# Two-layer graph network on one core: the check for uncovered edges stands behind the first two chunks' weights

## The chip, the cores and the metric

The kernel runs on one core of one Trainium2 chip. The metric is the device time of one execution in microseconds (us). An engine is named as the profile names it: PE is TensorE (PEld its weight loads), DVE VectorE, ACT ScalarE, POOL GpSimd, SP SyncE, the last used here only to start transfers. A "q" behind a name (DVEq, ACTq) is that engine's instruction queue: loads of registers, waits, issuing of transfers.

## The reference

There are 3,125 nodes of 64 numbers and 53,125 edges, sorted by their destination node. Two layers follow each other, each with a batch norm, a residual and a layer norm behind it:

```
layer 0: xj  = x[src]                                       # gather by edge
         B   = 8 spline weights per edge, from edge_attr_3
         agg = segment_sum((B (x) xj) @ W[8*64, 64], dst)   # by destination node
         x1  = layernorm(x + elu(batchnorm(agg / count(dst) + x @ root)))
layer 1: agg = segment_sum(x1[src] + edge_attr_64, dst)
         h   = relu(agg @ W1 + b1) @ W2 + b2
         out = layernorm(x1 + batchnorm(h))
```

## The kernel before

The edges lie in 416 tiles of 128; 8 tiles are a chunk (52 chunks), 2 chunks a pair (26 pairs). Since the edges are sorted, the 128 edges of a tile end in few neighbouring nodes: the kernel takes a window of 12 nodes from the first destination of each tile (`base`), and for pairs of tiles a window of 20 nodes. Whether each real edge lies in its window is checked at run time; if one doesn't, every engine takes a slow path at the end of layer 0 (`with ...If(flag > 0)`). With these inputs it isn't taken.

**The start.** SP loads sources, destinations and edge attributes; DVE casts them, PE transposes them (`turn_rows`, L382) so that an edge lies on a partition, DVE makes from them the columns the loop needs: `rel`, `comb`, `srcp` and `turn`. Then comes the check (L818 to L837): some 12 operations of DVE into `missed`, their row sums into `missed_row`, one matmul of PE that adds these over the partitions (L401), and a cast of the sum into `missed_any` (L837), which sets `flag_ready`. Behind it DVE computes the eight spline weights (`basis`, L841 to L851), clears a few tiles (L896 to L903) and builds the one-hot tiles of chunks 0 and 1: `pair` (L877), `ohp` (L880) and `whot` (L863, L867). PE and ACT wait for `flag_ready` before their loops.

**The loop over chunks.** Five engines work side by side, held together by semaphores:

- POOL gathers the rows `x[src]` of each tile by an indirect DMA (`gather_chunk`, L342), in four slots of one chunk each. The 32 gathers of chunks 0 to 3 are written out; a loop over chunks 4 to 15 (L348) and one over 16 to 51 (L351) follow. POOL waits for the list of indices of each pair (`idx_ready`), for the slot (`z_done`), and from chunk 16 on, before each half chunk, for `zsb_ready`, which ACT's copies L656 count up.
- SP loads the rows of `edge_attr_64` into the same slots (L291).
- PE runs `chunk`: per tile a matmul that counts pairs of nodes for layer 1 (L419, with a carry L425 every second tile) and the main matmul `z` (L470) over gathered rows and `whot`; once in a chunk it takes the previous chunk's `z` through the eight kernels (L432, L438), and at its end it counts edges (L443) and turns a tile of `x` or takes it through `root` (L407, L411).
- ACT copies the counted pairs out (`keep_pairs`, L647) and `z` (`keep_z`, L656). At the end of a pair it copies the list of indices for the pair two ahead (`lay_out`, L617). Behind pair 0 it enters its own loop (L676).
- DVE runs `two_chunks`: the one-hot tiles of the chunk two ahead, and `add_windows` (L892), which adds each tile's 12 columns into `agg` at an offset loaded into a register (L885). DVE waits through `m_ready` for PE's matmuls before it overwrites a `pair` tile.

**Behind the loop** PE folds `agg` (L526), DVE and ACT do the batch norm, ELU and layer norm of layer 0, PE does the 300 matmuls of layer 1's sum (L553, L558) while DVE ORs the counts in `adj` to look for an overflow (L1080), and the two last matrices, batch norm and layer norm of layer 1 end the kernel.

The order on each engine is the order in which the code is written. Temporary tiles of the start lie in the space of `adj` (`place`), which ACT fills with counted pairs from its first L647 on. `u` is layer 1's input; until layer 1 its columns hold `xroot` and `xt` and are unused above them.

Of the kernel before, what the change touches and what calls it, by code (L numbers as in the profile page):

```python
# [16 lines left out]
def gnn_two_layers(nc, x, src, dst, ea3, ea64, wk_d, root_d, gamma0, beta0,  # L17
                   w1_d, b1_d, w2_d, b2_d, gamma1, beta1, out):
    P = 128
# [56 lines left out]
    with ctx:  # L76
        def sb(name, shape, dt=F32):
            return ctx.enter_context(nc.sbuf_tensor(name, shape, dt))

        def sem(name):  # L80
            return ctx.enter_context(nc.semaphore(name))
# [14 lines left out]


        place = adj[:, :, :].rearrange("p t w -> p (t w)").bitcast(F32)
        sizes = [BLK * P * D, BLK * P, BLK * P, D * T * 2, T * 4, T, T, T, T, T, T,
                 BLK * P, BLK * P]  # L100
        ends = [sum(sizes[:n + 1]) for n in range(len(sizes))]
        lead = NT * NA // 4 - ends[-1]
        (ea3_rows, src_rows_f, dst_rows_f, w_lohi, w_pair, real, missed, missed2, srcf, srcj, steps_bad,
         src_rows, dst_rows) = (
            place[:, lead + e - n:lead + e] for n, e in zip(sizes, ends))
        ea3_rows = ea3_rows.rearrange("p (b e d) -> p b e d", b=BLK, e=P)
# [15 lines left out]
        hid = rows[:, :, :, :].rearrange("p s t c -> p (s t c)")[:, 0:N]  # L122
        xroot = u[0:PN, 0:(NT + 1) * C].rearrange("p (t c) -> p t c", c=C)
        xt = u[0:C, (NT + 1) * C:(NT + 1) * C + PN]
        x_now = sb("x_now", [PN, C])
        zero = sb("zero", [P, 1])
        ident = sb("ident", [P, P])
# [55 lines left out]
        base_ready = sem("base_ready")  # L183
# [192 lines left out]
        def _(pe):  # L376
# [20 lines left out]
            for d in range(D):  # L397
                turn_rows(ps[:, (0, 1, 7)[d], :], lambda b: ea3_rows[:, b, :, d], ea3_turned)

            pe.wait_ge(missed_ready, 1)  # L400
            nc.tensor.matmul(ps[0:1, 5, 0:1], missed_row[:, 0:1], ones[:, 0:1],  # L401
                             start=True, stop=True).then_inc(missed_summed, 1)

            pe.wait_ge(flag_ready, 1)

            def turn_x():
                nc.tensor.transpose(xt_ps, x_now[:, :], ident[0:PN, 0:PN]).then_inc(xt_turned, 1)  # L407

# [81 lines left out]

            for s in range(SLOTS):
                chunk(0, s, first=(s == 0))
            with pe.Fori(1, NCH // SLOTS) as i:
                for s in range(SLOTS):
                    chunk(i, s)
# [112 lines left out]
        def _(act):  # L608
# [12 lines left out]
            lay_out(CH, CH, CH)  # L621
            for n in range(1, AHEAD // STEP):
                lay_out(n * IDXS, n * IDXS)
            act.wait_ge(flag_ready, 1)

            def copy_x(i):
                nc.scalar.copy(x_now[:, :], x_nm[:, bass.ds(i, 1), :].rearrange("p t c -> p (t c)")).then_inc(x_copied, 1)
# [52 lines left out]
            def copy_fb_idx(layer):  # L680
                with act.Fori(0, T) as t:
                    act.wait_ge(fb_added[layer], t * NR + 1)
                    nc.scalar.copy(fb_idx[:, 0:1], src_col[:, bass.ds(t, 1)]).then_inc(fb_idx_ready[layer], 1)
                    if layer == 0:
                        with act.Fori(0, NR) as r:
# [74 lines left out]
        def _(dve):  # L760
            steps = [0]

            def then_wait(instruction):
                steps[0] += 1
                instruction.then_inc(dve_step, 1)
                dve.wait_ge(dve_step, steps[0])
# [23 lines left out]
            nc.vector.tensor_copy(base[0:1, 0:T], ps[0:1, 5, 0:T])  # L790
# [11 lines left out]
            nc.vector.scalar_tensor_tensor(out=srcp[:, 0:T], in0=srcj[:, :], scalar=-float(PN), in1=srcf[:, :],  # L802
                                           op0=ALU.mult, op1=ALU.add)

            dve.wait_ge(base_ready, 1)
            dve.wait_ge(dst_col_ready, 1)
            dve.wait_ge(base_spread, 1)
            then_wait(nc.vector.tensor_tensor(rel[:, 0:T], dst_col[:, :], ps[:, 6, 0:T], ALU.subtract))  # L810
            group_rel = missed2.rearrange("p (g n) -> p g n", n=GROUP)
            then_wait(nc.vector.tensor_tensor(
                group_rel, dst_col[:, :].rearrange("p (g n) -> p g n", n=GROUP),
                ps[:, 6, 0:T].rearrange("p (g n) -> p g n", n=GROUP)[:, :, 0:1].to_broadcast([P, G, GROUP]),
                ALU.subtract))
            then_wait(nc.vector.scalar_tensor_tensor(out=comb[:, 0:T], in0=srcj[:, :], scalar=float(GWIN),
                                                     in1=missed2[:, :], op0=ALU.mult, op1=ALU.add))
            then_wait(nc.vector.tensor_scalar(real[:, :], dst_col[:, :], 0.0, None, ALU.is_ge))  # L818
            nc.vector.scalar_tensor_tensor(out=missed[:, :], in0=rel[:, 0:T], scalar=0.0, in1=real[:, :],
                                           op0=ALU.is_lt, op1=ALU.mult)  # L820
            nc.vector.tensor_tensor(missed2[:, :], dst_col[:, :], ps[:, 4, 0:T], ALU.is_gt)
            group_step = steps_bad[0:1, 0:G]
            then_wait(nc.vector.tensor_tensor(group_step, base_f[0:1, GROUP:T + 1:GROUP], base_f[0:1, 0:T:GROUP],
                                              ALU.subtract))
            then_wait(nc.vector.tensor_scalar(turn[0:1, :], group_step, 0.0, float(GWIN - 1), ALU.max, ALU.min))
            then_wait(nc.vector.tensor_scalar(group_step, group_step, float(GWIN - 1), None, ALU.is_gt))
            then_wait(nc.vector.tensor_tensor(missed[0:1, 0:G], missed[0:1, 0:G], group_step, ALU.add))
            then_wait(nc.vector.tensor_tensor(srcf[0:1, :], base_f[0:1, 1:T + 1], base_f[0:1, 0:T], ALU.subtract))
            then_wait(nc.vector.tensor_tensor(missed[:, :], missed[:, :], missed2[:, :], ALU.add))
            nc.vector.tensor_scalar(steps_bad[0:1, :], srcf[0:1, :], 1.0, None, ALU.is_lt)  # L830
            then_wait(nc.vector.tensor_scalar(srcf[0:1, :], srcf[0:1, :], float(WIN - 1), None, ALU.is_gt))
            then_wait(nc.vector.tensor_tensor(missed[0:1, :], missed[0:1, :], steps_bad[0:1, :], ALU.add))
            then_wait(nc.vector.tensor_tensor(missed[0:1, :], missed[0:1, :], srcf[0:1, :], ALU.add))
            then_wait(nc.vector.tensor_tensor(missed[0:1, 0:1], missed[0:1, 0:1], base_f[0:1, 0:1], ALU.add))
            nc.vector.reduce_sum(missed_row[:, :], missed[:, :], axis=AX.X).then_inc(missed_ready, 1)
            dve.wait_ge(missed_summed, 1)
            nc.vector.tensor_copy(missed_any[0:1, 0:1], ps[0:1, 5, 0:1]).then_inc(flag_ready, 1)  # L837

            for d in range(D):
                dve.wait_ge(ea3_turned, d + 1)  # L840
# [60 lines left out]
            nc.vector.memset(ln_sum[:, :], 0.0).then_inc(xroot_ready, 1)  # L901
            nc.vector.memset(t_ps, 0.0).then_inc(t_ready, 2)
            then_wait(nc.vector.tensor_copy(iota_p, iota_f[:, 0:WIN]))  # L903
            for c in range(STEP):
                for half in range(2):
                    build_pairs(c, c, half)
                build_weights(c, c)

            def two_chunks(i, first=False):
                for par in range(STEP):  # L910
                    c, after, before = i * STEP + par, i * STEP + (par + STEP), i * STEP + (par - 1)
                    adds = not (first and par == 0)
# [229 lines left out]
```

## Time and profile before

| | |
|---|---|
| median of 3 runs | 677.46 us (676.99 to 678.1) |
| the profiled execution's own time | 677.0 us |
| its span in the profile, first to last instruction | 675.2 us |
| busy: PE, DVE, POOL, ACT | 511.0, 464.3, 399.1, 221.9 us |
| first main matmul on PE | 37.90 us |
| last gather issued by POOL | 529.47 us |
| first matmul of L526, behind the loop | 547.54 us |

No engine is busy for more than 76% of the span. So the shares alone don't say what bounds the kernel; that takes each engine's waits, stretch by stretch. Times in the rows below are from the span's start.

### The profile page before, as it was taken

The page shows a single profiled execution, that of the slowest core. Times are in us where ns is not written, and L with a number is a line of the kernel's source. Part 1 is how long each engine was busy: PE and PEld are TensorE (multiplying, and loading weights), DVE is VectorE, ACT ScalarE, POOL GpSimd, SP SyncE. Part 2 cuts the span into 40 slices and gives each one's busy share as a digit, 9 for nine tenths or more (in the row PEclk, how much of TensorE's full clock was granted, in tenths as well). Part 3 has the DMA queues.
Part 4 walks back from the last instruction along what each step waited for, and adds up shares of the span by engine and source line. Part 5 has one row for each costly group of instructions (what it writes and reads, how often), then busy time and mean ns, then how long its engine had stood idle before and what let it go on. Part 6 is the DMA issues. An engine that isn't in the chain of part 4 may idle for free.

```text
span 675.2 us, 14457 instructions
## 1 busy us (share of the span) xinstructions
PE 511.0 (76%) x3051; PEld 378.7 (56%) x3052; DVE 464.3 (69%) x1606; ACT 221.9 (33%) x478; POOL 399.1 (59%) x423
## 2 busy tenths in 40 slices
PE   5087888788879777888778877888788864699940
PEld 2065766566657556666556656666565663244530
DVE  6996666766766676766666667566666637889376
ACT  4033433433343333333333333333334203410421
POOL 6866777777777777777777777777777400000000
PEclk9996956876697788857885788777868755799975
DMA  5422221212221222122122122122211000000002
GB/s 119 97 61 54 60 58 44 68 45 58 56 58 43 56 56 58 41 58 56 43 56 55 44 58 57 43 56 58 56 41 25 18 2 0 1 1 0 1 1 48
DMA packets 77647, 30.58 MB, mean 45 GB/s; under 512 B 69598, under 2 KB 70971, under 8 KB 77627
## 3 DMA queue, kind: packets, MB, share of 16 engines
q1 hardware_dynamic: 63275, 16.69, 10.7%
q0 software_dynamic: 13312, 13.66, 9.3%
q8 instruction: 8, 0.13, 0.1%
q10 hardware_dynamic: 1040, 0.00, 0.1%
q14 instruction: 12, 0.10, 0.0%
HBM read 29.50 MB, written 0.80 MB: 45 GB/s over the span
## 4 chain that ended last, share of the span: by engine, by line
DVE 27%; PE 27%; issue 17%; POOL 11%; DVEq 11%; DMA 3%; ACT 2%; ACTq 1%; SPq 0%; POOLq 0%
POOL rows L342 11%; PE ps L470 9%; PE ps L419 8%; DVEq L885 7%; DVE agg L892 5%; DVE ohp L880 4%; DVE pair L1080 3%; DMA rows<-in_x,idx 3%; PE ps L438 2%; DVE pair L877 2%; PE ps L526 2%; DVE whot L867 2%; DVE pair L979 1%; DVEq L892 1%; PE ps L558 1%
## 5 line engine op out<-in xcount | busy, mean ns | idle before, releaser
L342 POOL DMA_INDIRECT rows<-in_x,idx x416 | 397.9, 957 | 133.2 <-issue 120.7
L470 PE MATMUL ps<-whot,rows 128*128 128x108 f32 x832 | 224.9, 362 | 74.2 <-DVE whot L867 31.6
L470 PEld LDWEIGHTS ps<-whot,rows 128*128 128x128 f32 x832 | 187.8, 256 | 118.3 <-issue 51.4
L419 PE MATMUL ps<-pair,ohp 128*125 128x500 bf16 x418 | 206.2, 494 | 24.0 <-DVE ohp L880 13.4
L647 ACT CAST adj<-ps 125x500 f32 x208 | 123.7, 595 | 245.6 <-PE ps L425 208.4
L877 DVE TENSOR_SCALAR pair<-iota_h,comb 128x500 bf16<-128x500 int16 x432 | 133.7, 371 | 66.5 <-issue 48.0
L892 DVE TENSOR_TENSOR agg<-agg,ps 128x24 f32 x416 | 74.8, 180 | 93.1 <-issue 41.9
L419 PEld LDWEIGHTS ps<-pair,ohp 128*125 128x125 bf16 x418 | 71.9, 172 | 37.9 <-issue 23.0
L880 DVE TENSOR_SCALAR ohp<-iota_h,srcp 128x125 bf16<-128x125 int16 x432 | 80.9, 277 | 0.0
L867 DVE TENSOR_TENSOR whot<-ps,basis 128x864 f32<-128x864 f32 x54 | 57.1, 1057 | 7.6
L438 PE MATMUL ps<-z_sb,wk 64*64 64x96 f32 x832 | 59.7, 298 | 0.0
L656 ACT COPY z_sb<-ps 128x432 f32<-128x432 f32 x104 | 54.2, 521 | 0.0
L438 PEld LDWEIGHTS ps<-z_sb,wk 64*64 64x64 f32 x832 | 47.6, 168 | 8.8 <-issue 5.7
L425 PE MATMUL ps<-pair,ohp 128*125 x208 | 48.2, 232 | 0.0
L553 PE MATMUL ps<-adj,basis 125*128 125x500 fp8e4 (+1 forms) x175 | 35.0, 362 | 11.0 <-ACT basis L730 11.0
L425 PEld LDWEIGHTS ps<-pair,ohp 128*125 128x125 bf16 x208 | 36.7, 176 | 10.0 <-issue 8.7
L553 PEld LDWEIGHTS ps<-adj,basis 125*128 125x128 bf16 x175 | 16.4, 100 | 29.5 <-ACT basis L730 11.2
L432 PE MATMUL ps<-z_sb,ident 128*64 128x96 f32 x104 | 25.3, 337 | 1.1 <-ACT z_sb L656 1.1
L1080 DVE TENSOR_TENSOR pair<-pair,adj 125x787 int32<-125x787 int32 x23 | 22.5, 978 | 0.8
L640 ACT COPY u<-ps 125x64 f32 (+1 forms) x26 | 5.5, 212 | 48.8 <-PE ps L411 48.8
L631 ACT COPY u<-ps 64x125 f32<-64x125 f32 x26 | 6.7, 258 | 37.2 <-PE ps L407 37.2
L432 PEld LDWEIGHTS ps<-z_sb,ident 128*64 128x64 f32 x104 | 12.9, 176 | 9.1 <-issue 5.5
(148 smaller groups left out, 317.2 us busy)
## 6 DMA issues: line engine op xcount, KB each, us to landing
rows<-in_edge_attr SPq DMA_DIRECT2D x51, 256.0 KB
rows<-in_x,idx POOLq DMA_INDIRECT x416, 2.4
x_nm<-in_x SPq DMA_DIRECT2D x1, 781.2 KB
out<-u SPq DMA_DIRECT2D x3, 218.8 KB
adj<-in_edge_attr SPq DMA_DIRECT2D x1, 576.0 KB
rows<-in_edge_attr SPq DMA_DIRECT2D x1, 224.0 KB
adj<-in_src SPq DMA_DIRECT2D x1, 192.0 KB
adj<-in_dst SPq DMA_DIRECT2D x1, 192.0 KB
```

The costliest lines, as they stand in the source:

```text
L342: pool.indirect_dma_start(rows[:, s, t, 0:C], None, x, bass.IndirectOffsetOnAxis(ap=idx[:, s * CH + t:s * CH + t + 1], axis=0)).then_inc(g ...
L419: return nc.tensor.matmul(m_ps[0:PN, g % MB, 0:PAIRS], ohp[:, par, t, :], pair[:, par, t, :], start=(n == 0), stop=(n == GROUP - 1), skip_ ...
L425: nc.tensor.matmul(m_ps[0:PN, (g + 1) % MB, 0:PAIRS].rearrange("p (j w) -> p j w", w=GWIN)[:, :, 0], ohp[:, par, t, :], bass.AP(pair, offs ...
L438: last = nc.tensor.matmul(t_ps[low:low + C, par, 0:RW], wk[:, k, :], z_of[0:C, :, k, :], start=(k < 2), stop=(k >= NK - 2))
L470: last = nc.tensor.matmul(z_ps[:, half, at:at + ZW], rows[:, s, t, :], whot[:, par, t, :], start=True, stop=True)
L553: nc.tensor.matmul(ps[:, b, 0:min(AB, N - b * AB)], table[:, j, 0:P], adj_part(b, j), start=(j == 0), stop=False, skip_group_check=True)
L647: nc.scalar.copy(bass.AP(adj, offset=start, ap=[[NT * NA, PN], [NA, NT], [1, GWIN]]), m_ps[0:PN, g % MB, 0:PAIRS].rearrange("p (j w) -> p ...
L656: nc.scalar.copy(z_sb[:, par, half * n:(half + 1) * n, :, :], z_ps[:, half, 0:n * ZW].rearrange("p (w k n) -> p w k n", w=n, k=KIN)).then_ ...
L867: nc.vector.tensor_tensor(whot[:, par, :, :].rearrange("p t (k w) -> p t k w", k=KIN), hot[:, :, :].rearrange("p t (a w) -> p t a w", a=1) ...
L877: nc.vector.tensor_scalar(pair[:, par, t, :], iota_h[:, :], comb[:, bass.ds(c * CH + t, 1)], None, ALU.is_equal)
L880: last = nc.vector.tensor_scalar(ohp[:, par, t, :], iota_h[:, 0:PN], srcp[:, bass.ds(c * CH + t, 1)], None, ALU.is_equal)
L892: nc.vector.tensor_tensor(view, view, t_ps[:, par, 0:2 * RW].rearrange("p (a w) -> p a w", a=2)[:, :, t * WIN:(t + 1) * WIN], ALU.add).the ...
```

## The change

The check leaves the start of DVE's stream. What the loop needs (`rel`, `comb`, `turn`) stays. One operation of the check stays as well, since it reads PSUM that is overwritten later: the comparison of the destinations with the next tile's base, now into `beyond`. The rest stands behind `whot` of chunk 1, before DVE's first `two_chunks`, and writes into `check`, three rows of 416 columns in the unused part of `u`. Three pairs of operations on the steps between bases are each joined into one `scalar_tensor_tensor`. PE's matmul over the partitions is issued behind chunk 1, into bank 7; the cast into `missed_any` behind DVE's first `two_chunks`. PE no longer waits for the flag ahead of its loop but behind it; ACT waits ahead of its loop for `base_kept` instead, and for the flag behind it.

```diff
@@ gnn_two_layers
+        check = u[:, (NT + 1) * C + PN:(NT + 1) * C + PN + 3 * T].rearrange("p (n t) -> p n t", n=3)
+        missed, beyond, real = check[:, 0, :], check[:, 1, :], check[:, 2, :]
@@ tensor
-            pe.wait_ge(missed_ready, 1)
-            nc.tensor.matmul(ps[0:1, 5, 0:1], missed_row[:, 0:1], ones[:, 0:1],
-                             start=True, stop=True).then_inc(missed_summed, 1)
-
-            pe.wait_ge(flag_ready, 1)
...
             for s in range(SLOTS):
                 chunk(0, s, first=(s == 0))
+                if s == 1:
+                    pe.wait_ge(missed_ready, 1)
+                    nc.tensor.matmul(ps[0:1, 7, 0:1], missed_row[:, 0:1], ones[:, 0:1],
+                                     start=True, stop=True).then_inc(missed_summed, 1)
...
+            pe.wait_ge(flag_ready, 1)
             flag = pe.value_load(missed_any[0:1, 0:1], min_val=0, max_val=1 << 30)
@@ scalar
-            act.wait_ge(flag_ready, 1)
+            act.wait_ge(base_kept, 1)
...
+            act.wait_ge(flag_ready, 1)
             flag = act.value_load(missed_any[0:1, 0:1], min_val=0, max_val=1 << 30)
@@ vector
-            then_wait(nc.vector.tensor_tensor(rel[:, 0:T], dst_col[:, :], ps[:, 6, 0:T], ALU.subtract))
+            nc.vector.tensor_tensor(rel[:, 0:T], dst_col[:, :], ps[:, 6, 0:T], ALU.subtract).then_inc(rel_ready, 1)
...
-            then_wait(nc.vector.tensor_scalar(real[:, :], dst_col[:, :], 0.0, None, ALU.is_ge))
-            nc.vector.scalar_tensor_tensor(out=missed[:, :], in0=rel[:, 0:T], scalar=0.0, in1=real[:, :],
-                                           op0=ALU.is_lt, op1=ALU.mult)
-            nc.vector.tensor_tensor(missed2[:, :], dst_col[:, :], ps[:, 4, 0:T], ALU.is_gt)
+            nc.vector.tensor_tensor(beyond[:, :], dst_col[:, :], ps[:, 4, 0:T], ALU.is_gt).then_inc(beyond_ready, 1)
...
-            then_wait(nc.vector.tensor_scalar(group_step, group_step, float(GWIN - 1), None, ALU.is_gt))
-            then_wait(nc.vector.tensor_tensor(missed[0:1, 0:G], missed[0:1, 0:G], group_step, ALU.add))
-            then_wait(nc.vector.tensor_tensor(srcf[0:1, :], base_f[0:1, 1:T + 1], base_f[0:1, 0:T], ALU.subtract))
-            then_wait(nc.vector.tensor_tensor(missed[:, :], missed[:, :], missed2[:, :], ALU.add))
-            nc.vector.tensor_scalar(steps_bad[0:1, :], srcf[0:1, :], 1.0, None, ALU.is_lt)
-            then_wait(nc.vector.tensor_scalar(srcf[0:1, :], srcf[0:1, :], float(WIN - 1), None, ALU.is_gt))
-            then_wait(nc.vector.tensor_tensor(missed[0:1, :], missed[0:1, :], steps_bad[0:1, :], ALU.add))
-            then_wait(nc.vector.tensor_tensor(missed[0:1, :], missed[0:1, :], srcf[0:1, :], ALU.add))
-            then_wait(nc.vector.tensor_tensor(missed[0:1, 0:1], missed[0:1, 0:1], base_f[0:1, 0:1], ALU.add))
-            nc.vector.reduce_sum(missed_row[:, :], missed[:, :], axis=AX.X).then_inc(missed_ready, 1)
-            dve.wait_ge(missed_summed, 1)
-            nc.vector.tensor_copy(missed_any[0:1, 0:1], ps[0:1, 5, 0:1]).then_inc(flag_ready, 1)
...
                 build_weights(c, c)
+            dve.wait_ge(rel_ready, 1)
+            dve.wait_ge(beyond_ready, 1)
+            then_wait(nc.vector.tensor_scalar(real[:, :], dst_col[:, :], 0.0, None, ALU.is_ge))
+            then_wait(nc.vector.scalar_tensor_tensor(out=missed[:, :], in0=rel[:, 0:T], scalar=0.0, in1=real[:, :],
+                                                     op0=ALU.is_lt, op1=ALU.mult))
+            then_wait(nc.vector.tensor_tensor(missed[:, :], missed[:, :], beyond[:, :], ALU.add))
+            steps_of_tiles, steps_of_groups = beyond[0:1, :], real[0:1, 0:G]
+            nc.vector.tensor_tensor(steps_of_tiles, base_f[0:1, 1:T + 1], base_f[0:1, 0:T], ALU.subtract)
+            then_wait(nc.vector.tensor_tensor(steps_of_groups, base_f[0:1, GROUP:T + 1:GROUP], base_f[0:1, 0:T:GROUP],
+                                              ALU.subtract))
+            for steps_in, n, bound, op in ((steps_of_tiles, T, 1, ALU.is_lt), (steps_of_tiles, T, WIN - 1, ALU.is_gt),
+                                           (steps_of_groups, G, GWIN - 1, ALU.is_gt)):
+                then_wait(nc.vector.scalar_tensor_tensor(out=missed[0:1, 0:n], in0=steps_in, scalar=float(bound),
+                                                         in1=missed[0:1, 0:n], op0=op, op1=ALU.add))
+            then_wait(nc.vector.tensor_tensor(missed[0:1, 0:1], missed[0:1, 0:1], base_f[0:1, 0:1], ALU.add))
+            nc.vector.reduce_sum(missed_row[:, :], missed[:, :], axis=AX.X).then_inc(missed_ready, 1)
...
             two_chunks(0, first=True)
+            dve.wait_ge(missed_summed, 1)
+            nc.vector.tensor_copy(missed_any[0:1, 0:1], ps[0:1, 7, 0:1]).then_inc(flag_ready, 1)
```

On DVE at the start, this is the stream before, from the group window into `comb` (L812, L816) to the first operation of the spline weights (L841); `adj` stands for every temporary in its space:

```order
L812 TENSOR_TENSOR adj<-dst_col,ps 128x416
L816 SCALAR_TENSOR_TENSOR comb<-adj 128x416
L818 TENSOR_SCALAR adj<-dst_col 128x416
L819 SCALAR_TENSOR_TENSOR adj<-rel,adj 128x416
L821 TENSOR_TENSOR adj<-dst_col,ps 128x416
L823 TENSOR_TENSOR adj<-base_f 1x208
L825 TENSOR_SCALAR turn<-adj 1x208
L826 TENSOR_SCALAR adj<-adj 1x208
L827 TENSOR_TENSOR adj<-adj 1x208
L828 TENSOR_TENSOR adj<-base_f 1x416
L829 TENSOR_TENSOR adj<-adj 128x416
L830 TENSOR_SCALAR adj<-adj 1x416
```

The same place of the stream now, where L824 is the first operation of the spline weights:

```order
L811 TENSOR_TENSOR adj<-dst_col,ps 128x416
L815 SCALAR_TENSOR_TENSOR comb<-adj 128x416
L817 TENSOR_TENSOR u<-dst_col,ps 128x416
L818 TENSOR_TENSOR adj<-base_f 1x208
L820 TENSOR_SCALAR turn<-adj 1x208
L824 TENSOR_SCALAR adj<-ps 128x416 x3
```

L818 and L819 of before are gone from here, and so is all from L826 to L837, six more operations and the cast behind the seven shown: 13 instructions, and the trip over PE.

On DVE behind the weights of chunk 1 (L850, L867 before), ahead of the one-hot tiles of chunk 2 (L860, L877 before), this is what stands there now:

```order
L850 TENSOR_TENSOR whot<-ps,basis 128x864
L897 TENSOR_SCALAR u<-dst_col 128x416
L898 SCALAR_TENSOR_TENSOR u<-rel,u 128x416
L900 TENSOR_TENSOR u<-u 128x416
L902 TENSOR_TENSOR u<-base_f 1x416
L903 TENSOR_TENSOR u<-base_f 1x208
L907 SCALAR_TENSOR_TENSOR u<-u 1x416 x2
L907 SCALAR_TENSOR_TENSOR u<-u 1x208
L909 TENSOR_TENSOR u<-u,base_f 1x1
L910 TENSOR_REDUCE missed_row<-u 128x1
L860 TENSOR_SCALAR pair<-iota_h,comb 128x500 x4
```

Before, L867 was followed at once by L877; now ten operations stand between them.

## Rows read from the trace of the kernel before

**Rows 1.** Part 5 of the page, POOL's gathers (columns as in its head: busy, mean ns).
```profile
L342 POOL DMA_INDIRECT rows<-in_x,idx x416 | 397.9, 957 | 133.2 <-issue 120.7
```
**Rows 2.** Waits: engine line waited for: us in total, times, longest us.
```profile
POOL rows L342 <- ACT idx L617: 5.8, 4, 4.9
...
PE ps L470 <- DMA rows<-in_x,idx: 15.8, 14, 2.4
```
**Rows 3.** Timeline of POOL: start us, us, engine line op, [idle before <-releaser].
```profile
46.77 0.94 POOL L342 DMA_INDIRECT rows<-in_x,idx  x1 [0.31 <-issue]
52.58 0.94 POOL L342 DMA_INDIRECT rows<-in_x,idx  x1 [4.87 <-ACT idx L617]
...
72.59 0.94 POOL L342 DMA_INDIRECT rows<-in_x,idx  x1 [0.30 <-issue]
...
172.73 0.94 POOL L342 DMA_INDIRECT rows<-in_x,idx  x1 [0.30 <-issue]
...
187.82 0.95 POOL L342 DMA_INDIRECT rows<-in_x,idx  x1 [0.30 <-issue]
...
529.47 0.94 POOL L342 DMA_INDIRECT rows<-in_x,idx  x1 [0.31 <-issue]
```
**Rows 4.** Timeline of PE: the last half chunk's wait for gathered rows.
```profile
535.43 0.47 PE L470 MATMUL ps<-whot,rows 128*128 128x108 f32 x2 [2.08 <-DMA rows<-in_x,idx]
```
**Rows 5.** Timeline of DVE at the start.
```profile
14.33 0.38 DVE L818 TENSOR_SCALAR adj<-dst_col 128x416 f32<-128x416 f32 x1
14.74 0.60 DVE L819 SCALAR_TENSOR_TENSOR adj<-rel,adj 128x416 f32<-128x416 f32 x1
15.25 0.58 DVE L821 TENSOR_TENSOR adj<-dst_col,ps 128x416 f32<-128x416 f32 x1
...
16.55 0.26 DVE L826 TENSOR_SCALAR adj<-adj 1x208 f32<-1x208 f32 x1
...
21.53 1.56 DVE L841 TENSOR_SCALAR adj<-ps 128x416 f32<-128x416 f32 x3
```
**Rows 6.** Timeline of PE from the start to the end of chunk 2.
```profile
13.09 3.34 PE L382 MATMUL ps<-ident,adj 128*128 128x128 f32 x12 [0.78 <-DMA adj<-in_edge_attr]
...
37.90 0.73 PE L470 MATMUL ps<-whot,rows 128*128 128x108 f32 x2 [1.58 <-issue]
...
45.12 0.38 PE L419 MATMUL ps<-pair,ohp 128*125 128x500 bf16 x1
...
51.22 0.42 PE L419 MATMUL ps<-pair,ohp 128*125 128x500 bf16 x1
...
56.19 0.65 PE L419 MATMUL ps<-pair,ohp 128*125 128x500 bf16 x1 [3.81 <-ACT adj L647]
...
64.46 0.62 PE L419 MATMUL ps<-pair,ohp 128*125 128x500 bf16 x1
```
**Rows 7.** Windows: us, busy PE, PEld, DVE, ACT, POOL, PEclk, DMA share, GB/s.
```profile
44.46:54.70 10.24, 7.64 (x62) 6.14 (x60) 8.02 (x35) 3.79 (x10) 4.46 (x5) 1.00 0.30 70
54.70:64.94 10.24, 8.75 (x43) 6.97 (x44) 4.89 (x23) 3.34 (x8) 7.65 (x9) 0.50 0.13 27
```
**Rows 8.** Timeline of ACT around the ends of pairs 0, 1 and 2, and chunk 15's copy.
```profile
51.43 0.21 ACT L617 COPY idx<-src_col 128x16 int32<-128x16 int32 x1
55.47 0.57 ACT L647 CAST adj<-ps 125x500 f32 x1 [3.83 <-issue]
...
71.34 0.20 ACT L617 COPY idx<-src_col  x1
...
85.27 0.20 ACT L617 COPY idx<-src_col  x1
...
185.31 0.52 ACT L656 COPY z_sb<-ps 128x432 f32<-128x432 f32 x1
```
**Rows 9.** Timeline of DVE behind the weights of chunk 1, and at its loop.
```profile
42.75 1.32 DVE L877 TENSOR_SCALAR pair<-iota_h,comb 128x500 bf16<-128x500 int16 x4
...
59.63 1.13 DVE L877 TENSOR_SCALAR pair<-iota_h,comb 128x500 bf16<-128x500 int16 x4 [3.23 <-issue]
```

More of the change, by code:

```diff
@@ L98, in gnn_two_layers @@
         place = adj[:, :, :].rearrange("p t w -> p (t w)").bitcast(F32)
-        sizes = [BLK * P * D, BLK * P, BLK * P, D * T * 2, T * 4, T, T, T, T, T, T,
+        sizes = [BLK * P * D, BLK * P, BLK * P, D * T * 2, T * 4, T, T, T, T,
                  BLK * P, BLK * P]
@@ L102, in gnn_two_layers @@
         lead = NT * NA // 4 - ends[-1]
-        (ea3_rows, src_rows_f, dst_rows_f, w_lohi, w_pair, real, missed, missed2, srcf, srcj, steps_bad,
+        (ea3_rows, src_rows_f, dst_rows_f, w_lohi, w_pair, in_group, srcf, srcj, group_steps,
          src_rows, dst_rows) = (
@@ L182, in gnn_two_layers @@
         src_col_ready, dst_col_ready, basis_in = sem("src_col_ready"), sem("dst_col_ready"), sem("basis_in")
-        base_ready = sem("base_ready")
+        base_ready, base_kept, rel_ready, beyond_ready = sem("base_ready"), sem("base_kept"), sem("rel_ready"), sem("beyond_ready")
         base_spread, missed_ready, missed_summed, flag_ready = (
@@ L789, in _ @@
             nc.vector.tensor_copy(base_f[0:1, 0:T], ps[0:1, 5, 0:T]).then_inc(base_ready, 1)
-            nc.vector.tensor_copy(base[0:1, 0:T], ps[0:1, 5, 0:T])
+            nc.vector.tensor_copy(base[0:1, 0:T], ps[0:1, 5, 0:T]).then_inc(base_kept, 1)
             nc.vector.tensor_copy(dst_col[:, :], ps[:, 5, 0:T]).then_inc(dst_col_ready, 1)
@@ L809, in _ @@
             dve.wait_ge(base_spread, 1)
-            then_wait(nc.vector.tensor_tensor(rel[:, 0:T], dst_col[:, :], ps[:, 6, 0:T], ALU.subtract))
-            group_rel = missed2.rearrange("p (g n) -> p g n", n=GROUP)
+            nc.vector.tensor_tensor(rel[:, 0:T], dst_col[:, :], ps[:, 6, 0:T], ALU.subtract).then_inc(rel_ready, 1)
             then_wait(nc.vector.tensor_tensor(
-                group_rel, dst_col[:, :].rearrange("p (g n) -> p g n", n=GROUP),
+                in_group.rearrange("p (g n) -> p g n", n=GROUP), dst_col[:, :].rearrange("p (g n) -> p g n", n=GROUP),
@@ L814, in _ @@
                 ps[:, 6, 0:T].rearrange("p (g n) -> p g n", n=GROUP)[:, :, 0:1].to_broadcast([P, G, GROUP]),
                 ALU.subtract))
-            then_wait(nc.vector.scalar_tensor_tensor(out=comb[:, 0:T], in0=srcj[:, :], scalar=float(GWIN),
-                                                     in1=missed2[:, :], op0=ALU.mult, op1=ALU.add))
-            then_wait(nc.vector.tensor_scalar(real[:, :], dst_col[:, :], 0.0, None, ALU.is_ge))
-            nc.vector.scalar_tensor_tensor(out=missed[:, :], in0=rel[:, 0:T], scalar=0.0, in1=real[:, :],
-                                           op0=ALU.is_lt, op1=ALU.mult)
@@ L821, in _ @@
-            nc.vector.tensor_tensor(missed2[:, :], dst_col[:, :], ps[:, 4, 0:T], ALU.is_gt)
-            group_step = steps_bad[0:1, 0:G]
-            then_wait(nc.vector.tensor_tensor(group_step, base_f[0:1, GROUP:T + 1:GROUP], base_f[0:1, 0:T:GROUP],
-                                              ALU.subtract))
-            then_wait(nc.vector.tensor_scalar(turn[0:1, :], group_step, 0.0, float(GWIN - 1), ALU.max, ALU.min))
-            then_wait(nc.vector.tensor_scalar(group_step, group_step, float(GWIN - 1), None, ALU.is_gt))
@@ L832, in _ @@
-            then_wait(nc.vector.tensor_tensor(missed[0:1, :], missed[0:1, :], steps_bad[0:1, :], ALU.add))
-            then_wait(nc.vector.tensor_tensor(missed[0:1, :], missed[0:1, :], srcf[0:1, :], ALU.add))
-            then_wait(nc.vector.tensor_tensor(missed[0:1, 0:1], missed[0:1, 0:1], base_f[0:1, 0:1], ALU.add))
-            nc.vector.reduce_sum(missed_row[:, :], missed[:, :], axis=AX.X).then_inc(missed_ready, 1)
-            dve.wait_ge(missed_summed, 1)
-            nc.vector.tensor_copy(missed_any[0:1, 0:1], ps[0:1, 5, 0:1]).then_inc(flag_ready, 1)
+            nc.vector.scalar_tensor_tensor(out=comb[:, 0:T], in0=srcj[:, :], scalar=float(GWIN),
+                                           in1=in_group[:, :], op0=ALU.mult, op1=ALU.add)
@@ L839, in _ @@
+            nc.vector.tensor_tensor(beyond[:, :], dst_col[:, :], ps[:, 4, 0:T], ALU.is_gt).then_inc(beyond_ready, 1)
+            then_wait(nc.vector.tensor_tensor(group_steps[0:1, 0:G], base_f[0:1, GROUP:T + 1:GROUP], base_f[0:1, 0:T:GROUP],
+                                              ALU.subtract))
+            then_wait(nc.vector.tensor_scalar(turn[0:1, :], group_steps[0:1, 0:G], 0.0, float(GWIN - 1), ALU.max, ALU.min))
             for d in range(D):
@@ L903, in _ @@
             then_wait(nc.vector.tensor_copy(iota_p, iota_f[:, 0:WIN]))
+            dve.wait_ge(base_kept, 1)
             for c in range(STEP):
```

## The prediction

> **What bounds the kernel now.** I read the costliest groups first. POOL's gathers are one kind of instruction, 416 of them, busy for 397.9 us, with 120.7 us of short gaps between them [rows 1]. So each takes 0.957 + 0.30 = 1.25 us of POOL's stream, 520 us in all: of the 547.5 us until PE begins with L526, the gathers alone need nearly everything. The waits say whether POOL ever stops: for ACT's list of indices it waited 5.8 us in all, and 4.9 of them in one piece [rows 2]. The timeline places that piece: gather 32 starts at 46.77, gather 33 at 52.58, with 4.87 us idle ahead of it [rows 3]. From there to the last gather at 529.47 are 383 steps in 476.89 us, 1.245 us each: no further stop. And PE waits for that stream: 15.8 us in 14 waits for gathered rows [rows 2], the last of them 2.08 us ahead of the last half chunk, until 535.43 [rows 4]. Hence the end of the loop follows POOL, and POOL's stream has one hole. What is won ahead of the loop comes out at the end only as far as gather 33 starts earlier, and as later waits of POOL allow it.
>
> **The start.** In before, 14.33 to 15.25 goes to L818 and L819 (0.92), and 16.55 to 21.53 to everything from L826 to the cast behind the trip over PE (4.98) [rows 5]. Both go: 5.90 us. Edits in what stays (two waits fewer) I set at nothing; they could give up to 0.1. The spline weights then start at 15.63. They read what PE has turned by 13.09 + 3.34 = 16.43 [rows 6]; the three reads lie about 0.5 apart (1.56 for three), the third comes at 16.6 and is not held. Everything up to the one-hot tiles of chunk 0 moves by 5.9, and so does PE's first main matmul, which waits for `whot`: 37.90 becomes 32.0.
>
> **Chunks 0 and 1 on PE.** Chunk 0 takes 45.12 - 37.90 = 7.2 us and would end at 39.2. Chunk 1 took 51.22 - 45.12 = 6.1 [rows 6], nearly all at the higher of the two clock levels: the granted clock is 1.00 (2.4 GHz) in 44.46 to 54.70 and 0.50 (1.2 GHz) in 54.70 to 64.94 [rows 7]. At the lower level six of the eight tiles of chunk 2, with the kernels, took 64.46 - 56.19 = 8.27 [rows 6]; by chunk 0's 0.9 a tile less what stands around it, I estimate a whole chunk at 9.3. Does PE get its higher level at the same instant, though it begins 5.9 us earlier? I assume the same instant, 44.46, as the cautious case. Then 39.2 to 44.46 does 5.26/9.3 = 57% of chunk 1, and the other 43% takes 2.6: end at 47.1, 4.1 earlier than 51.22. Bounds: with the rise earlier too, 45.3 (5.9 earlier); with none, 48.5 (2.7 earlier).
>
> **Gather 33.** The list for pair 2 is ready at 51.43 + 0.21 = 51.64 [rows 8], 4.1 earlier at 47.5 (45.7 to 48.9). POOL itself is through with gather 32 at 47.71 and would start the next at 48.02. Before, 0.94 passed between list and gather [rows 3, 8]; whether that is the wake or part of the loop's entry can't be seen. Between 48.02 and 48.5 I take 48.5: 4.1 earlier than 52.58. Bounds 4.56 (POOL's own pace) and 2.7.
>
> **Gather 49, the next one at risk.** The list for pair 3 was ready at 71.54, 1.05 ahead of gather 49 at 72.59 [rows 3, 8]. Gather 49 would now come at 68.5, so the list must be there by some 68.2, 3.3 earlier. PE's pause until 56.19 waits for ACT, which sat 3.83 us idle on its way into its loop behind L617 [rows 6, 8]; that pause moves with L617, to 52.1. From there to ACT's L617 at 71.34 were 15.15 us, of which 8.75 at the lower level and 6.4 at the higher: 8.75/1.5 + 6.4 = 12.2 us of work at the higher level (9.3/6.1 = 1.5). With the levels at their old instants, 52.1 to 54.70 does 2.6, 54.70 to 64.94 does 6.8, and 2.8 remain: L617 at 67.7, ready at 67.9. Just in time. If the lower level lasted to the end of pair 1 it would be 70.4, and gather 49 would start at about 70.8, 1.8 earlier than before.
>
> **DVE's new piece.** Ten instructions stand between the weights of chunk 1 and the one-hot tiles of chunk 2. From the rows of before [rows 5]: a comparison of 416 columns 0.41 to the next start; six operations of 416 columns with two inputs (the first product, the add, the steps between tiles, two joined ones, the row sums) at 0.60, the longest of those rows, 3.6; two of 208 columns at 0.3 (0.26 and a short gap); one of a single element at 0.2. Together 4.8; with the wait at the head I take 4.9 us. DVE reaches it 5.9 earlier, so the one-hot tiles of chunk 2, at 42.75 before [rows 9], start at 41.8: 1.0 earlier still, so no later than before. PE reaches them 4.1 to 5.9 earlier and could have to wait, but it stands anyway until 52.1 for ACT, and DVE's 1.0 is inside of that. From there on DVE is late in the queue. It began its loop's first tiles at 59.63 behind 3.23 us of idling [rows 9], part of it PE's pause; that idling takes up about 1.4 of the lag. So PE and DVE go into the loop 1 to 3 us ahead of before, POOL 4.1. Who waits for whom there? POOL, from chunk 16 on, waits for ACT's copies of z: the tightest of those waits is before gather 141, at 187.82, whose copy was done at 185.83, 1.99 ahead [rows 3, 8]. With POOL 4.1 earlier it needs the loop 2.1 earlier. I take that as met. Cost of DVE's piece: nothing; without its cover, up to 1 us at gather 141. The matmul behind chunk 1 and the cast behind DVE's first `two_chunks` cost some 0.2 and 0.15, inside the same pauses.
>
> **A rule that speaks against the gain.** Entering the loop at L348 is a taken branch. ACT sat 3.83 us idle on entering its loop, DVE 3.23 [rows 8, 9]; POOL's entry lies in the very 4.87 us that I count as a wait for indices. POOL's second loop begins with gather 129, at 172.73, and there the gap is the usual 0.30 [rows 3]. By the second loop POOL's entry is free, and the sum stands.
> The Trainium skill (Runtime: NRT & Kernel Launch, Instruction fetch mechanics) says that a taken branch to a target outside the pages already held makes the engine fetch the page before it goes on. ACT's idling agrees with it and POOL's second loop doesn't.
>
> **Sum.** 677.0 of the profiled execution less 4.1 = 672.9. Its 677.0 stands 0.46 below the median of before's runs, 677.46; against that median the same gain gives 673.4. Behind the loop nothing is changed: the flag is set hundreds of microseconds ahead. I forecast 673.4; the mechanism's own range is 672.8 (4.6 gained) to 674.5 (3.0).
>
> **Rivals.**
> 1. *Gather 49 or 141 waits.* The lower level of PE's clock, or DVE's lag, holds the loop back and POOL stops a second time. For it: the margins are 1.05 and 1.99 [rows 3, 8]. Against: both need the loop ahead by only 2 to 3 us, out of 5.9. Gain 1.8 to 3.0: about 675.2.
> 2. *The hole is POOL's loop entry.* Then gather 33 comes ACT's 3.3 us (3.83 less its load) behind 47.71, at 51.2, and the gain is 1.4: 676.1, on the edge of no change. For it ACT and DVE, against it the second loop.
> 3. *DVE's piece is the new bound, and the kernel is slower.* If the ten operations, with their waits, took over 7.9 us instead of 4.9, the loop would start more than 2.0 later than before, gather 141 would wait, and each further microsecond would come out at the end. At 10 us, the double, it is 2.1 slower: 679.6. For it: nothing in the rows exceeds 0.60 an operation. Against: ten times the longest row is 6.0.
>
> **How the numbers follow.** Forecast 60%, rival 1 20%, rival 2 11%, rival 3 4%; the other 5% are for what the later clock levels do behind the loop, either way. What a measurement can tell here is 0.2%, 1.35 us. Faster by more: the forecast and rival 1 whole, half of rival 2, half of the rest: 0.87. Within: half of rival 2, a little of rival 3: 0.08. Slower: 0.05. The range leaves out rival 3, the far half of rival 2, and gains over 5.7: 671.8 to 676.0.
>
> **What would show it.** Spline weights at 15.6; first main matmul at 32.0; ten operations of 4.9 us in DVE's stream from 36.9 to 41.8; gather 33 at 48.0 to 48.5; gathers 49 and 141 with the usual gap of 0.30; the last gather near 525.4, the last wait for its rows still there, and L526 at 543.4. Wrong, if POOL's gap ahead of gather 33 stays above 1 us, if another gap over 0.5 us turns up behind it, or if the stretch from the last gather to the end grows by more than 1 us.

## The result: 673.6 us, 4 us faster

| | before | changed |
|---|---|---|
| median | 677.46 us (5 runs, 676.99 to 678.10) | 673.6 us (5 runs, 672.96 to 675.98) |
| profiled execution, span | 677.0, 675.2 us | 672.96, 671.1 us |
| gather 33 / last gather starts | 52.58 / 531.97 us | 48.12 / 527.47 us |
| first matmul behind the loop | 547.54 us | 543.04 us |

The ratio is 0.9948, 95% interval 0.9928 to 0.9969. The forecast was 673.4, in a range of 671.8 to 676.0. Gathers are counted from 1 in the order in which POOL issues them: 1 to 32 are those of chunks 0 to 3, gather 33 is the first of chunk 4.

Two numbers ahead of the prediction are wrong. The first: the last gather of the kernel before starts at 531.97, not at 529.47. The row at 529.47 [rows 3] is the last but two. The stream then gives 383 steps in 479.39 us, 1.252 us each, much as the costliest group had it (0.957 + 0.30); the argument is not touched. The second: between `comb` and the spline weights five more operations and the cast went behind the seven shown, not six; 13 instructions is right.

In the profile after, POOL's waits have no long one left (engine line waited for: us in total, times, longest us). They answer to [rows 2].

```profile
POOL rows L344 <- issue: 117.6, 386, 0.3
POOL rows L344 <- ACT z_sb L657: 7.9, 26, 0.3
POOL rows L344 <- DMA idx<-in_src: 2.2, 1, 2.2
...
POOL rows L344 <- ACT idx L618: 0.9, 3, 0.3
```

POOL's timeline after (start us, us, engine line op, [idle before <-releaser]) shows gathers 32, 33, 49 and the last one, each 1.25 us behind the one before it (no gather behind the first has a gap over 0.31 us ahead of it); they answer to [rows 3]:

```profile
46.88 0.94 POOL L344 DMA_INDIRECT rows<-in_x,idx  x1 [0.30 <-issue]
48.12 0.94 POOL L344 DMA_INDIRECT rows<-in_x,idx  x1 [0.30 <-issue]
...
68.11 0.95 POOL L344 DMA_INDIRECT rows<-in_x,idx  x1 [0.30 <-issue]
...
527.47 0.94 POOL L344 DMA_INDIRECT rows<-in_x,idx  x1 [0.30 <-issue]
```

The hole of 4.87 us is gone. Gather 33 is 4.46 earlier, the last gather 4.50, L527 behind the loop 4.50: what was won at gather 33 arrives at the loop's end unchanged. The last wait for gathered rows is still there (530.92, 2.41 us, with 535.43 and 2.08 before [rows 4]).

DVE's timeline after, at the start and behind the weights of chunk 1, answers to [rows 5] and [rows 9]:

```profile
15.08 0.34 DVE L820 TENSOR_SCALAR turn<-adj 1x208 int32<-1x208 f32 x1
15.46 1.58 DVE L824 TENSOR_SCALAR adj<-ps 128x416 f32<-128x416 f32 x3
...
36.07 0.42 DVE L897 TENSOR_SCALAR u<-dst_col 128x416 f32<-128x416 f32 x1
...
40.50 0.59 DVE L910 TENSOR_REDUCE missed_row<-u 128x1 f32<-128x416 f32 x1
41.00 1.21 DVE L860 TENSOR_SCALAR pair<-iota_h,comb 128x500 bf16<-128x500 int16 x4
42.14 0.73 DVE L863 TENSOR_SCALAR ohp<-iota_h,srcp 128x125 bf16<-128x125 int16 x4
```

The spline weights start 6.07 earlier; the ten operations take 4.93, from 36.07 to 41.00. PE's timeline after answers to [rows 6]:

```profile
33.98 0.76 PE L466 MATMUL ps<-whot,rows 128*128 128x108 f32 x2 [3.98 <-DMA rows<-in_edge_attr]
...
40.41 0.38 PE L415 MATMUL ps<-pair,ohp 128*125 128x500 bf16 x1
...
44.95 0.37 PE L415 MATMUL ps<-pair,ohp 128*125 128x500 bf16 x1
...
46.63 0.42 PE L415 MATMUL ps<-pair,ohp 128*125 128x500 bf16 x1
...
51.40 0.65 PE L415 MATMUL ps<-pair,ohp 128*125 128x500 bf16 x1 [3.62 <-ACT adj L648]
```

The first main matmul is at 33.98, not 32.0: `whot` was there at 31.2, but the matmul now waits for SP's load of chunk 0's edge attributes. Chunk 1 (40.41 to 46.63) nevertheless ends 4.6 earlier: 3.9 of it is PE's earlier start, and chunk 0 takes 6.4 instead of 7.2 us, because the higher clock level is granted from 38.90 on instead of 44.46. The window answers to [rows 7], with its columns:

```profile
38.90:49.14 10.24, 8.62 (x69) 7.00 (x69) 9.13 (x34) 4.40 (x11) 8.04 (x8) 1.00 0.39 79
```

ACT's timeline after gives the lists for pairs 2 and 3; they answer to [rows 8]:

```profile
46.72 0.21 ACT L618 COPY idx<-src_col 128x16 int32<-128x16 int32 x1
...
66.43 0.20 ACT L618 COPY idx<-src_col  x1
```

The lists are there at 46.93 and 66.63, 1.19 and 1.48 ahead of their gathers.

Of the 4.5 us at the loop's end, 4.1 are left in the span. The other 0.4 go on PE behind the loop, most of it in layer 1's sum (L554, L553 before). Here are the windows from the sum's first matmul to the rise of the clock in both kernels. The columns are those of [rows 7]: before,

```profile
580.59:583.77 3.18, 3.18 (x9) 1.29 (x10) 2.81 (x7) 0.88 (x2) 0.00 (x0) 0.50 0.02 5
```

and after:

```profile
576.10:581.62 5.52, 5.52 (x15) 2.14 (x16) 5.01 (x11) 2.01 (x4) 0.00 (x0) 0.50 0.01 3
```

The sum begins 4.49 earlier, but it runs 5.52 instead of 3.18 us at 1.2 GHz before 2.4 GHz is granted. Half of the extra 2.3 us is work lost: the sum's second part begins only 3.35 earlier, in before and after:

```profile
615.49 8.41 PE L558 MATMUL ps<-adj,basis 125*64 125x500 fp8e4 x75
```

```profile
612.14 8.41 PE L559 MATMUL ps<-adj,basis 125*64 125x500 fp8e4 x75
```

PE had 0.8 in hand, since it waited that long for the overflow check of DVE before, so 0.3 are lost by the sum's end (L564 is 4.23 earlier than L563 was). The remaining 0.2 go in the batch norm behind it, where one pair of PE's matmuls (L538 at 642.96) takes 0.62 instead of 0.43 us at the lower level. Nothing ties this to the change: in the ten profiled executions outside e1 to e4 (before, changed, e5 to e8, f1 to f4) the rise came 2.8 (f1) to 5.6 us (f4) behind the sum's first matmul, and in no order that follows the edits.

### The profile page after: what moved, and what is told of

Read it like the earlier page. It is cut to its first block, busy times and chain, and to the rows that moved or that the text cites. A ratio compares the mean times of both kernels' runs of the same rounds, so it can differ in the third digit from the quotient of the medians.

```text
span 671.1 us, 14458 instructions
## 1 busy us (share of the span) xinstructions
PE 505.5 (75%) x3051; PEld 377.1 (56%) x3052; DVE 463.7 (69%) x1604; ACT 222.4 (33%) x478; POOL 399.1 (59%) x423
## 4 chain that ended last, share of the span: by engine, by line
PE 32%; DVE 24%; issue 16%; DVEq 11%; POOL 10%; DMA 3%; ACT 2%; ACTq 0%; SPq 0%; POOLq 0%
POOL rows L344 10%; PE ps L466 9%; DVEq L868 7%; PE ps L415 7%; PE ps L554 5%; DVE agg L875 5%; DVE ohp L863 4%; DVE pair L860 4%; DMA rows<-in_x,idx 3%; PE ps L434 3%; PE ps L559 2%; DVE whot L850 2%; PE ps L527 2%; DVE pair L984 1%; DVEq L875 1%
## 5 line engine op out<-in xcount | busy, mean ns | idle before, releaser
L860 DVE TENSOR_SCALAR pair<-iota_h,comb 128x500 bf16<-128x500 int16 x432 | 133.7, 371 | 63.0 <-issue 41.2
L850 DVE TENSOR_TENSOR whot<-ps,basis 128x864 f32<-128x864 f32 x54 | 57.1, 1058 | 7.6
L434 PE MATMUL ps<-z_sb,wk 64*64 64x96 f32 x832 | 58.3, 294 | 0.0
L554 PE MATMUL ps<-adj,basis 125*128 125x500 fp8e4 (+1 forms) x175 | 36.1, 370 | 11.1 <-ACT basis L732 11.1
L554 PEld LDWEIGHTS ps<-adj,basis 125*128 125x128 bf16 x175 | 16.7, 102 | 30.3 <-ACT basis L732 11.2
L559 PE MATMUL ps<-adj,basis 125*64 125x500 fp8e4 (+1 forms) x175 | 17.5, 353 | 0.0
```

Source lines behind the costliest of these rows:

```text
L434: last = nc.tensor.matmul(t_ps[low:low + C, par, 0:RW], wk[:, k, :], z_of[0:C, :, k, :], start=(k < 2), stop=(k >= NK - 2))
L554: nc.tensor.matmul(ps[:, b, 0:min(AB, N - b * AB)], table[:, j, 0:P], adj_part(b, j), start=(j == 0), stop=False, skip_group_check=True)
L850: nc.vector.tensor_tensor(whot[:, par, :, :].rearrange("p t (k w) -> p t k w", k=KIN), hot[:, :, :].rearrange("p t (a w) -> p t a w", a=1) ...
L860: nc.vector.tensor_scalar(pair[:, par, t, :], iota_h[:, :], comb[:, bass.ds(c * CH + t, 1)], None, ALU.is_equal)
```

## The experiments

Theory A: the loop's end follows POOL's stream of gathers, and the gain is the closed hole ahead of gather 33. Theory B: the gain is PE's and DVE's earlier start. Each ratio is against runs of the kernel before on the same chip; times of runs on different chips are best compared through their ratios.

| run | what | median us | ratio to before, 95% | gather 33 / last gather |
|---|---|---|---|---|
| f1_hole_back | changed, POOL held | 682.81 | 1.0089 (1.0073 to 1.0106) | 58.10 / 538.08 |
| f2_no_check | changed, no check | 674.08 | 0.9958 (0.9942 to 0.9975) | 47.98 / 528.39 |
| f3_check_double | changed, 5.5 us more on DVE | 677.41 | 1.0015 (1.0003 to 1.0028) | 52.04 / 532.13 |
| e5_check_first | changed, check at DVE's start | 675.4 | 0.9972 (0.9962 to 0.9983) | 50.47 / 530.39 |
| e6_lists_early | before, lists early | 674.94 | 0.9963 (0.9949 to 0.9977) | 48.61 / 531.39 |
| e7_lists_lead6 | e6 and later gate | 674.32 | 0.9957 (0.9940 to 0.9973) | 49.01 / 528.69 |
| e8_edges_first | changed, SP's load first | 674.38 | 0.9953 (0.9935 to 0.9970) | 47.84 / 528.42 |
| f4_after_lists | changed and e7 | 673.32 | 0.9948 (0.9932 to 0.9965) | 48.06 / 527.51 |

Across these eight runs, and the kernels before and after, one figure hardly moves: the span ends 142.9 to 144.2 us behind the start of the last gather, whether that gather starts at 527.47 or at 538.08.

**e1 to e4: the same kernels on a chip where POOL isn't the bound.** On a first chip ran the changed kernel unaltered (e1_again) and three others (e2_hole_back, e3_no_check, e4_check_double), the kernels that f1, f2 and f3 below repeat.

> The changed kernel once more, unaltered. Theory A (the end of the loop follows POOL's stream of gathers, and the gain is the closed hole ahead of gather 33): 4 us under the kernel before, about 673.6, first main matmul at 34.0, POOL never idle for more than 0.31 us between gathers behind number 1. Theory B (the gain is PE's and DVE's earlier start, and POOL's hole was incidental): the same. It is the measure for the runs beside it and shows how far the changed kernel scatters (673.0 to 676.0 in five runs).

None of that came. There the kernel before took 932.14 us, e1 932.05 (ratio 1.0001, 0.9975 to 1.0027), e2 931.55 (0.998), e3 932.69 (1.0004), e4 933.38 (1.0001): no difference can be told between any of them. The waits of e1:

```profile
ACT adj L648 <- remote: 430.8, 43, 20.4
...
POOL rows L344 <- ACT z_sb L657: 179.1, 38, 12.0
...
DVE agg L875 <- remote: 175.6, 33, 14.3
```

ACT idles for something that the profile doesn't name ("remote"), 430.8 us in 43 waits, 10 us each, and POOL now waits 179.1 us for ACT: its gathers are no longer the bound, and earlier gathers bring nothing. What holds ACT on that chip stays open. These four runs decide nothing between A and B; that an earlier gather 33 is worth nothing where POOL stops anyway fits A.

**f1_hole_back: put the hole back, leave the early start.**

```diff
                 gather_chunk(0, s, in_step=False)
+            pool.wait_ge(z_done, 2 * SLOTS + 5)
             with nc.Fori(1, LEAD_TRIPS, ...
```

> The same kernel as e2_hole_back, once more beside a kernel before that takes 677 us: in the first job the kernel before itself took 932 us, and POOL stopped 12 to 15 us ahead of each pair's gathers in all four kernels, so its hole could not be told there. The changed kernel with POOL held ahead of gather 33 until the first half of chunk 2 is through PE. Theory A (the end follows POOL's stream): gather 33 at about 53.2 instead of 48.1, 5.0 slower than the changed kernel: 678.5. Theory B (PE's and DVE's head start is the gain): 673.6 to 674.5.

PE's last matmul of the awaited half chunk, and gather 33 on POOL:

```profile
53.70 0.74 PE L467 MATMUL ps<-whot,rows 128*128 128x108 f32 x2
```

```profile
58.10 0.94 POOL L344 DMA_INDIRECT rows<-in_x,idx  x1 [10.47 <-issue]
```

The release came at 54.4, 1.6 later than expected, and gather 33 another 3.7 later, at 58.10 where 53.2 was expected. It is 9.98 later than in the changed kernel, and the time is 9.5 us longer by the ratios (1.0089 less 0.9948), 8.7 against f2 on the same chip: close to one to one. PE began nearly as early as in the changed kernel (34.42), and the kernel is still slower than before. PE's early start alone wins nothing; theory B falls. The 3.7 us come back below.

**f2_no_check: is the moved check still paid for?** The ten operations are left out.

```diff
-            dve.wait_ge(rel_ready, 1)
...
-            nc.vector.reduce_sum(missed_row[:, :], missed[:, :], axis=AX.X).then_inc(missed_ready, 1)
+            nc.vector.memset(missed_row[:, :], 0.0).then_inc(missed_ready, 1)
```

> The same kernel as e3_no_check: the ten operations of the check are left out and missed_row is set to zero. Theory A: DVE's ten operations were covered, 673.6 within 0.5. Rival (they are still a cost on the path): 670 to 672.5.

674.08, and gather 33 at 47.98: 4.9 us less on DVE gain nothing that can be measured (0.9958 against 0.9948). The check is covered.

**f3_check_double: how far does the cover reach?**

```diff
-            then_wait(nc.vector.tensor_scalar(real[:, :], dst_col[:, :], 0.0, None, ALU.is_ge))
-            then_wait(nc.vector.scalar_tensor_tensor(out=missed[:, :], ...
+            for _ in range(6):
+                (the same two)
```

> The same kernel as e4_check_double: 5.2 us more of DVE behind the weights of chunk 1. Theory A: the loop follows DVE 5 later, POOL's margins (1.48 at gather 49's list, 1.58 at gather 149) are used up and a stop of 3 to 3.6 us turns up: 676.6 to 677.2. Rival (DVE's idling takes the lag up first): 673.6 to 674.5.

The piece measured 10.39 us instead of 4.93. It cost 4.5 us against the changed kernel's ratio (1.0015 less 0.9948, 0.67%), about a microsecond more than expected, and not where I had looked for it. DVE, PE, ACT and POOL in order of time:

```profile
47.31 0.73 DVE L863 TENSOR_SCALAR ohp<-iota_h,srcp 128x125 bf16<-128x125 int16 x4
```

```profile
48.10 0.42 PE L415 MATMUL ps<-pair,ohp 128*125 128x500 bf16 x1 [3.17 <-DVE ohp L863]
```

```profile
50.89 0.21 ACT L618 COPY idx<-src_col 128x16 int32<-128x16 int32 x1
```

```profile
52.04 1.05 POOL L344 DMA_INDIRECT rows<-in_x,idx  x1 [4.29 <-ACT idx L618]
```

PE counts the first tiles of chunk 2 at the end of chunk 1, ahead of the list for pair 2. So DVE's lateness goes through PE and ACT straight into gather 33. In the changed kernel DVE has those tiles at 42.14 + 0.73 = 42.87 and PE takes them at 44.95: 2.1 us of cover. Here they came 5.2 later, and 3.17 showed up on PE. The pause cost more than itself: behind it the granted clock is 0.50 (48.5 to 50.9), where the changed kernel did the same work at 1.00, so that the list comes 4.2 later and gather 33 3.9. Another 0.7 goes at gather 133, which waited 0.99 us for ACT's copy of z; together that is the 4.66 by which the last gather is later.

**e5_check_first: only the place.** The sixteen lines of the check, as in the change, ahead of the loop over `ea3_turned`.

```diff
             then_wait(nc.vector.tensor_scalar(turn[0:1, :], group_steps[0:1, 0:G], ...
+            dve.wait_ge(rel_ready, 1)
...
+            nc.vector.reduce_sum(missed_row[:, :], missed[:, :], axis=AX.X).then_inc(missed_ready, 1)
             for d in range(D):
```

> The changed kernel with the whole check (in its new form, with its rows in u) at DVE's start again, ahead of the spline weights; PE's matmul and the cast stay behind chunk 1. It parts the place of the check from the shorter form and the missing trip over PE. Theory A and B: the start is 4.9 later than in the changed kernel, 1.0 earlier than before, gather 33 at about 51.5: 676.3. If the gain lay in the form or in PE and ACT no longer waiting for the flag, and not in the place: 673.6.

675.4, a gain of 0.28%, 1.9 us. POOL's hole is 3.36 us, and gather 33 is at 50.47, 2.1 earlier than before:

```profile
50.47 0.95 POOL L344 DMA_INDIRECT rows<-in_x,idx  x1 [3.36 <-ACT idx L618]
```

About half of the gain comes from the shorter form and from PE and ACT no longer waiting for the flag, the rest from the place. It is almost a microsecond more than expected; PE starts 1.5 earlier (36.40).

**e6_lists_early and e7_lists_lead6: close the hole without moving the check.**

```diff
-        idx = sb("idx", [P, AHEAD * CH], I32)
+        idx = sb("idx", [P, 2 * AHEAD * CH], I32)
...
+            for s in range(SLOTS):
+                gather_chunk(1, s, in_step=False, lists=AHEAD * CH)
-            with nc.Fori(1, LEAD_TRIPS, ...
+            with nc.Fori(2, LEAD_TRIPS, ...
...
+            for n in range(AHEAD // STEP, 2 * (AHEAD // STEP)):
+                lay_out(n * IDXS, n * IDXS)
```

e7 has `LEAD_TRIPS = 6` on top.

> The kernel before, with the check where it was, but the lists of indices for pairs 2 and 3 are laid out at the start into columns of their own, and the gathers of chunks 4 to 7 are written out, so that gathers 33 and 49 wait for no list. PE, ACT and DVE start as late as before. Theory A: gather 33 at 48.0, 4.5 earlier; later waits of POOL take a part back, since the loop is not ahead: gather 141 had 1.99 of margin, so 2.6 stop there and 2.0 remain: 675.5. Theory B: nothing gained, 677.5.

> The same as e6_lists_early, and POOL waits for ACT's copies of z only from chunk 24 on instead of chunk 16, where the margins of before were 5.7 and more. Theory A: the stop at gather 141 is gone, the whole 4.5 comes out without the check being moved: 673.0. Theory B: 677.5.

Gathers 129 and 141 of e6:

```profile
169.93 0.94 POOL L342 DMA_INDIRECT rows<-in_x,idx  x1 [1.46 <-ACT z_sb L660]
...
187.34 0.94 POOL L342 DMA_INDIRECT rows<-in_x,idx  x1 [2.61 <-ACT z_sb L660]
```

The stop at gather 141 is the one forecast from the margins of before; a second, at gather 129, is there too. The two stops (1.46 and 2.61 instead of 0.30) give back 3.5 of the 4.0 us won at gather 33 in this execution (its last gather is at 531.39; at 676.7 it is also the longest of five, the median is 674.94). e7 has no such stop; its gather 33:

```profile
49.01 0.94 POOL L342 DMA_INDIRECT rows<-in_x,idx  x1 [0.30 <-issue]
```

Its last gather is 3.28 earlier than before, with PE starting as late as before (37.67), and it takes 674.32, 3.1 less. So most of the gain can be had without the early start. It is 1.3 us short of the 673.0 expected; gather 33 came only 3.6 earlier, since gathers 1 to 32 took 1 us longer in all in that execution.

**e8_edges_first: start PE earlier still.**

```diff
+            sp.wait_ge(z_done, 2)
+            sp.dma_start(rows[:, 0, :, C:P], ea64_full[:, 0:CH, :]).then_inc(ea_loaded[0], 16)
             sp.dma_start(x_nm[:, 0:NT, :], node_major(x)).then_inc(x_loaded, 16)
...
-            with sp.Fori(0, NCH // SLOTS - 1) as i:
+            for s in range(1, SLOTS):
+                load_ea(s, s)
+            with sp.Fori(1, NCH // SLOTS - 1) as i:
```

> The changed kernel, with the load of chunk 0's edge attributes issued by SP ahead of x and the weights instead of behind them. The changed kernel's first main matmul waits 3.98 us for that load, until 33.98, though whot is there at 31.2. Here it should start at 31.3. Theory A: POOL has no hole left, so the time stays, 673.6. Theory B: PE starts 2.7 earlier, 671 to 672.5.

```profile
32.28 0.73 PE L470 MATMUL ps<-whot,rows 128*128 128x108 f32 x2 [1.36 <-issue]
```

The first main matmul moved to 32.28 and no longer waits for the load. That is 1.0 later than expected, since DVE's first one-hot tiles came 0.9 later in this execution. The time is 674.38: nothing gained, as A has it.

**f4_after_lists: all margins wide.** The edits of e6 and e7 on the changed kernel.

> The changed kernel with the early lists of e6_lists_early and the later gate of e7_lists_lead6 on top. Theory A: POOL had no stop left in the profiled run, so nothing is gained there, 673.0; but its margins of 1.5 us at gather 49 and 149 become wide, so that runs in which one of these waits bites (674.6 and 676.0 among the five of the changed kernel) should be gone: median 673.2, highest under 674. Rival (what scatters lies elsewhere, behind the loop or in the gathers' own pace): 673.6 with the same scatter.

673.32 (672.58 to 673.37). It is as fast as the changed kernel, at the same ratio. Four runs lie within 0.8 us, where the five of the changed kernel spread over 3.0. That the narrow margins cause the spread is not shown: the runs are few, and the four of f2 spread over only 1.3 on the same chip, with the changed kernel's lists and gate.

## Why the prediction was right

- *The bound.* Right, and shown by f1 (a gather 33 that is 9.98 us later cost 9.5), e7 and e8, and by the constant distance from the last gather to the end.
- *5.90 us at the start.* 6.07; the third turned block was no wait.
- *First main matmul at 32.0.* Wrong: 33.98. I followed `whot` alone. The matmul waits for SP's load as well, and behind a `whot` that came at 37.8 that load had never been the last. Its cost was hidden by the next point.
- *The clock's rise at 44.46 as before.* Wrong in the safe direction: it came at 38.90. The error on SP's load and this one cancelled: chunk 1 ended at 46.6, where I had 47.1. That was luck. With the matmul at 33.98 and the rise still at 44.46, the prediction's own reckoning gives 48.4 for the end of chunk 1 and 49.8 for gather 33, a gain of 2.8 and not 4.1 (an estimate from its rates of 9.3 and 6.1 us a chunk).
- *Gather 33 at 48.0 to 48.5.* 48.12, at POOL's own pace; list for pair 3 forecast at 67.9, found at 66.63. The last gather was forecast at 525.4 from the wrong row at 529.47; less the same 4.1, the right row gives 527.9, and it came at 527.47.
- *DVE's piece 4.9 us, covered.* 4.93, and covered (f2). The reason was half wrong: PE was said to stand until 52.1 anyway, but it needs the first tiles of chunk 2 before that pause, and the cover was 2.1 us there, not the margin at gather 141. The rival "DVE's piece is the new bound" named the wrong place, and from f3 also a wrong size: with 10.4 us of piece the kernel was 1.0 slower than before (0.2 to 1.9), where 10 us was to make it 2.1 slower. The cover was 2.1 us at PE and another 0.25 at gather 33 (its list was there at 46.93, and 0.94 later it could have started, at 47.87), so by my estimate a piece over some 7.3 us would have cost time already, and not first over 7.9.
- *Nothing changes behind the loop.* 0.4 us were lost there by the clock, inside the 5% left for it.
- *POOL's loop entry is free.* True here, and not for the reason given. f1 shows the price when POOL stands at the entry: 3.7 us. Of these some 0.94 may be the plain wake, since that much passes between list and gather where POOL waits inside its loop, in before, e5 and f3 alike. In the changed kernel nothing of it is seen. The sum of rival 2 is also off by 0.2: 47.71 and 3.3 make 51.0, a gain of 1.6.

## What to carry to other kernels

Where one engine issues a stream that takes nearly the whole span, look only for the holes in that stream, and follow from each hole backwards through every engine that releases it. What is shortened ahead of the loop counts up to the stream's own pace and no further. When work is moved behind the first releases, ask which engine takes the next tile of the mover, and when: here PE took it before the list that the stream waits for.

## What the runs showed of the hardware

- POOL, held ahead of its loop until 54.4 (f1), issued its first gather there 3.7 us later; where POOL had gathers in hand as it came there (changed kernel, [rows 3] at 172.73), the gap was the usual 0.30. ACT's idling on entering its own loop was 3.83 before and 3.75 after. The Trainium skill (Runtime: NRT & Kernel Launch, Instruction fetch mechanics) says that a taken branch outside the pages held forces a fetch before going on; f1 agrees with it. Its trace has two transfers of instructions on queue q14 between the release and gather 33, at 55.5 and 57.7, and none there from 30 to 49. The changed kernel has two at 34.1 and 36.7, between gathers, and none there from 38 to 48.3. The three kernels whose loop on POOL begins only behind gather 64 (e6, e7, f4) have none from 35 to 48 either. So the fetch passed while POOL was still busy with earlier gathers. That these pairs are POOL's is inferred from that, since the queue doesn't name the engine.
- PE's rise to 2.4 GHz came earlier with its work at the start (38.90 instead of 44.46, for matmuls beginning at 28.52 instead of 34.84). In layer 1's sum, which PE enters behind 11 us of idling, it came 3.2 us behind the first matmul before, 5.5 after, and 2.8 to 5.6 us in the ten profiled executions outside e1 to e4.
- The same program, the kernel before, took 932 us on one chip and 677 us on others.
